# A mixture-of-experts stage: first blocks at fixed places, padding from two hardware DMA queues, late weights and the Gelu table asked for early

## The reference, cut to what matters

```python
deg = max((adj != 0).sum(-1), 1)
x = x + relu((a_norm(adj, deg) @ ln(x) + ln(x)) @ W + b)          # graph layer
xf = ln(x)
logits = xf @ Wr + br                                             # 16 experts
topk_w, topk_idx = top_k(softmax(logits), 2); topk_w /= topk_w.sum()
for e in range(16):
    h = gelu(xf @ W1[e] + b1[e])          # 256 -> 512
    o = h @ W2[e] + b2[e]                 # 512 -> 256
    y = y + combine[:, e:e+1] * o
x = x + xf + y
```

## Time and profile before

| | |
|---|---|
| median of three runs | 675.21 us |
| the profiled execution: its time / its span | 674.82 us / 673.2 us |
| TensorE busy | 601.6 us (89%) |
| VectorE, GpSimd, ScalarE busy | 456.5, 351.9, 232.0 us |
| graph layer ends, about | 338 us |
| first block's transposes, T(0) | 362.97 us |
| mean granted TensorE clock | 0.970 |

### The profile page before, as it was taken

One profiled execution on the slowest core, in us unless ns is written; L12 is line 12 of the kernel. 1 busy time (PEld: TensorE's weight loads), 2 busy tenths in 40 slices (PEclk: granted clock), 3 DMA queues, 4 the chain that ended last, 5 costly groups with the idle time before them and its releaser, 6 DMA issues. The chain is left out here.

```text
span 673.2 us, 17554 instructions
## 1 busy us (share of the span) xinstructions
PE 601.6 (89%) x4798; PEld 464.8 (69%) x4799; DVE 456.5 (68%) x1372; ACT 232.0 (34%) x482; POOL 351.9 (52%) x390
## 2 busy tenths in 40 slices
PE   2999999999999999999924899998999999999993
PEld 1777888888888788888811566665667767677772
DVE  2755788888888888889871567675765566566561
ACT  2785333333323332323320343433333323332331
POOL 6232566666777566665457245444345344344443
PEclk9999999999999999999965899999999999999997
DMA  9908799999999999997274357656734443443410
GB/s 237 225 10 157 141 198 196 197 194 192 189 193 191 194 175 186 190 192 177 90 294 131 81 130 155 139 116 141 143 66 82 76 76 65 69 73 65 80 34 2
DMA packets 65918, 93.25 MB, mean 139 GB/s; under 512 B 9547, under 2 KB 40559, under 8 KB 65360
## 3 DMA queue, kind: packets, MB, share of 16 engines
q0 software_dynamic: 33696, 51.87, 46.0%
q1 hardware_dynamic: 31600, 39.76, 19.0%
q10 hardware_dynamic: 576, 1.05, 0.5%
HBM read 103.71 MB, written 25.83 MB: 192 GB/s over the span
## 5 line engine op out<-in xcount | busy, mean ns | idle before, releaser
L459 PE MATMUL bank<-wall,at_xg 128*128 128x257 f16 x1024 | 238.6, 274 | 5.9 <-DVE at_xg L801 5.8
L461 PE MATMUL bank<-wall,at_xg 128*128 128x256 f16 x1024 | 233.1, 273 | 0.0
L1272 POOL DMA_INDIRECT out_dram<-orows,at_xg x79 | 128.5, 1626 | 165.6 <-DMA out_dram<-orows,at_xg 112.5
L563 PE MATMUL bank<-wall,feat 128*128 x474 | 118.6, 387 | 10.9 <-issue 9.0
L459 PEld LDWEIGHTS bank<-wall,at_xg 128*128 128x128 f16 x1024 | 102.8, 100 | 27.9 <-DVE at_xg L801 13.8
L1100 DVE SCALAR_TENSOR_TENSOR hl<-bank,xseT 128x512 f16<-128x512 f32 x79 | 54.6, 691 | 92.2 <-ACT xseT L744 92.2
L1238 POOL DMA_INDIRECT rows<-feat,posi x64 | 66.8, 1044 | 91.1 <-issue 90.8
L738 ACT ACTIVATE hgs<-hgs 128x512 f32<-128x512 f32 x79 | 49.8, 630 | 185.4 <-DVE hgs L1094 185.4
L461 PEld LDWEIGHTS bank<-wall,at_xg 128*128 128x128 f16 x1024 | 100.3, 98 | 15.0
L586 PE MATMUL bank<-wall,xseT 128*128 x632 | 109.1, 274 | 0.0
L563 PEld LDWEIGHTS bank<-wall,feat 128*128 128x128 f16 x474 | 46.5, 98 | 59.1 <-issue 25.5
(11 more groups left out here) (149 smaller groups left out, 826.5 us busy)
## 6 DMA issues: line engine op xcount, KB each, us to landing
abuf<-in_adj_dram POOLq DMA_DIRECT2D x128, 256.0 KB, 6.6
wst<-in_L_ffn_W_dram SPq DMA_DIRECT2D x32, 512.0 KB, 4.7
at_xg<-rows SPq DMA_DIRECT2D x79, 136.0 KB, 2.4
out_dram<-orows SPq DMA_DIRECT2D x32, 128.0 KB
abuf<-in_L_ffn_b_dram SPq DMA_DIRECT2D x4, 1024.0 KB, 10.2
wall<-in_x_dram SPq DMA_DIRECT2D x12, 256.0 KB, 13.2
out_dram<-orows,at_xg POOLq DMA_INDIRECT x79
wall<-in_x_dram ACTq DMA_DIRECT2D x4, 256.0 KB, 6.3
```

The source lines that it names most:

```text
L459: both = [lambda: pe.matmul(ps_acc[odd][:, 0:D + 1], w, yh[:, j, 0:D + 1], start=j == 0, stop=j == T - 1), lambda: pe.matmul(ps_acc[odd][: ...
L461: lambda: pe.matmul(ps_acc[odd][:, 0:D], w, yl[:, j, :], start=False, stop=False)]
L563: mm = pe.matmul(q_h[r % 2][:, :], a, w, start=n == 0, stop=n == 3 * DC - 1)
L1272: L.indirect_dma_start(out, bass.IndirectOffsetOnAxis(ap=info[r][:, 0:1].bitcast(U32), axis=0), orow[r], None, bounds_check=N - 1, oob_is_ ...
```

## The change: what it does

Every expert's region grows by 128 rows (`ROOM = CAP + P`), so that a padding write of 128 rows always fits. The first eight blocks are the first blocks of experts 0 to 7, always, at row r x ROOM; an expert without tokens gets a block of pad rows. Their row and expert are constants in the program. The table covers only the 71 blocks after them. The padding is one plain DMA of 128 rows per expert, whose row is read from a register: experts 0 to 3 by SP, 4 to 7 and 8 to 15 by ScalarE. SP asks for the first two late weight transfers right behind its last store of the graph layer. ScalarE runs one tiny Gelu before its padding writes. The adds of the first eight blocks each wait for the add before.

```diff
-FIRST = 2
+PADS = ((0, 4), (4, 8), (8, 16))
+ROOM = CAP + P
+    def fixed(q):
+        return isinstance(q, int) and q == 0
+    def write_pads(eng, which):
+        eng.wait_ge(ev("counted_out"), 1)
+        for e in range(*PADS[which]):
+            at_place = eng.value_load(pad_at[0:1, e:e + 1], min_val=e * ROOM, max_val=e * ROOM + CAP)
+            eng.dma_start(rows[bass.ds(at_place, P), :], pad[:, :]).then_inc(padded[which], 16)
+    def after_pads(eng, which):
+        first, end = PADS[which]
+        eng.wait_ge(padded[which], 16 * (end - first))
# SP
-        sp.wait_ge(ev("table_made"), 1)
-        after(sp, "pads_table", 0)
-        for odd in (0, 1):
-            sp.wait_ge(listed[odd], 16 * TOPK * T // 2)
-        sp.wait_ge(ev("multiplied"), T * CH)
-        sp.wait_ge(ev("padded_first"), 16 * FIRST)
         def load_block(q, r):
             if not isinstance(q, int) or q > 0:
                 after_added(sp, q - 1, r)
+            if fixed(q):
+                row = r * ROOM
+            else:
                 passed(sp)
-            row = sp.value_load(tab[0:1, bass.ds(blk(q, r), 1)], ...)
-            pads = sp.value_load(pads_before[0:1, bass.ds(blk(q, r), 1)], ...)
-            sp.wait_ge(ev("padded"), pads)
-            passed(sp)
+                row = sp.value_load(tab[0:1, bass.ds(in_table(q, r), 1)], ...)
...
+            if is_block(nxt, 0, PADS[1][0]):
+                after_pads(sp, 1)
+            if is_block(nxt, 1, 0):
+                after(sp, "table_made", 0)
+                sp.wait_ge(ev("spare_pads"), 16)
+                after_pads(sp, 2)
...
         load_late(0)
         load_late(1)
+        write_pads(sp, 0)
+        for odd in (0, 1):
+            sp.wait_ge(listed[odd], 16 * TOPK * T // 2)
+        sp.wait_ge(ev("multiplied"), T * CH)
+        after_pads(sp, 0)
# TensorE, ahead of T(0)
-        pe.wait_ge(ev("table_made"), 1)
+        after(pe, "table_made", 0)
+        after(pe, "earlier_made", 0)
# ScalarE, behind the last tile
+        act.activation(warm[:, :], mhalf[:, 0:1], ACT.Gelu).then_inc(ev("gelu_warm"), 1)
+        write_pads(act, 1)
+        write_pads(act, 2)
# VectorE
+        V.tensor_copy(pad_at[:, :], ps_P[0:1, 0:E]).then_inc(ev("counted_out"), 1)
-        V.scalar_tensor_tensor(out=padi[:, :], in0=padf[:, 0, :], scalar=float(PLACES), in1=padf[:, 1, :], ...)
...
+        V.tensor_scalar(nblk[:, :], nblk[:, :], 0.0, None, ALU.max).then_inc(ev("table_step"), 1)
# GpSimd
-        for e in range(E):
-            L.indirect_dma_start(rows, ...padi[:, e:e + 1]..., pad[:, :], ...)
...
         def add_results(q, r):
             after(L, "weighted", blk(q, r))
             if not isinstance(q, int) or blk(q, r) >= 2:
                 after_added(L, *shift(q, r, -2))
-            if not isinstance(q, int) or blk(q, r) >= 1:
+            if fixed(q):
+                if r >= 1:
+                    L.wait_ge(added[(r + 1) % 2], 16 * ((r + 1) // 2))
+            else:
                 others = L.value_load(earlier[...], ...)
                 L.wait_ge(added[(r + 1) % 2], others)
```

More of the change, by code:

```diff
@@ L74 @@
 LATE = 4
-PLACES = E * CAP + P
+ROOM = CAP + P
+PLACES = E * ROOM + P
 RW = 272
@@ L161, in build @@
     rowinfo = feat[:, :, :, D:D + 2]
-    padf = sb("padf", [P, 2, E], F32)
-    padi = sb("padi", [P, E], I32)
+    pad_at = sb("pad_at", [1, E], I32)
+    warm = sb("warm", [P, 1], F32)
     base = [orows[:, 7 - k, :] for k in range(2)]
@@ L232, in build @@
     listed = [sem(f"listed{c}") for c in range(2)]
+    padded = [sem(f"padded{k}") for k in range(len(PADS))]
     xg_in = [sem(f"xg_in{c}") for c in range(U)]
@@ L318, in blk, with is_block, in_table @@
         return q * U + r
+    def fixed(q):
+        return isinstance(q, int) and q == 0
+    def is_block(at, q, r):
+        return isinstance(at[0], int) and at == (q, r)
+    def in_table(q, r):
+        return blk(q, r) - U
+    def write_pads(eng, which):
[6 more added lines that the diff above has]
+        eng.wait_ge(padded[which], 16 * (end - first))
     block = ctx.enter_context(nc.Block())
@@ L588, in expert_out @@
             mm.then_inc(ev("expert_out"), 1)
-        pe.wait_ge(ev("table_step"), 12)
-        after(pe, "pads_known", 0)
-        for k, c in enumerate((3, 4, 6)):
+        pe.wait_ge(ev("table_step"), 14)
+        for k, c in enumerate((3, 4)):
             mm = pe.matmul(ps_R[0:1, k * P:(k + 1) * P], tbl[:, c:c + 1], id32[:, :], start=True, stop=True)
@@ L1017, in _ @@
         V.wait_ge(ev("table_step"), 2)
-        V.tensor_scalar(padf[:, 0, :], cnt[:, :], 2.0 ** 23, float(P), ALU.subtract, ALU.mult).then_inc(ev("pad_step"), 1)
-        V.tensor_scalar(padf[:, 1, :], run[:, :], iota_p[:, 0:1], None, ALU.add).then_inc(ev("pad_step"), 1)
-        V.wait_ge(ev("pad_step"), 2)
-        V.tensor_tensor(padf[:, 0, :], padf[:, 1, :], padf[:, 0, :], ALU.is_ge).then_inc(ev("pad_step"), 1)
-        V.wait_ge(ev("pad_step"), 3)
-        V.scalar_tensor_tensor(out=padi[:, :], in0=padf[:, 0, :], scalar=float(PLACES), in1=padf[:, 1, :],
-                               op0=ALU.mult, op1=ALU.add).then_inc(ev("pads_placed"), 1)
         V.scalar_tensor_tensor(out=nblk[:, :], in0=cnt[:, :], scalar=2.0 ** 23, in1=first_block[:, :],
@@ L1067, in _ @@
         after(V, "earlier_step", 2)
-        V.tensor_scalar(tbl[:, 5:6], tbl[:, 5:6], 16.0, None, ALU.max).then_inc(ev("earlier_ready"), 1)
+        V.tensor_scalar(tbl[:, 5:6], tbl[:, 5:6], 16.0 * U / 2, None, ALU.add).then_inc(ev("earlier_ready"), 1)
         after(V, "earlier_T", 0)
@@ L1087, in expert_of @@
         def expert_of(q, r):
-            return V.value_load(tab[0:1, bass.ds(blk(q, r) + P, 1)], min_val=0, max_val=E - 1)
+            if fixed(q):
+                return r
+            return V.value_load(tab[0:1, bass.ds(in_table(q, r) + P, 1)], min_val=0, max_val=E - 1)
         def bias1(q, r, e):
@@ L1172, in _ @@
         L.tensor_copy(firsts[:, :], run[:, :]).then_inc(ev("constants"), 1)
-        L.iota(first_block[:, :], [[CAP // P, E]], base=0, channel_multiplier=0, allow_small_or_imprecise_dtypes=True)\
-         .then_inc(ev("constants"), 1)
+        for half in (0, 1):
+            L.iota(first_block[:, half * EARLY:E - EARLY + half * EARLY], [[ROOM // P, EARLY]],
+                   base=half * EARLY * ROOM // P + 1 - half, channel_multiplier=0,
+                   allow_small_or_imprecise_dtypes=True).then_inc(ev("constants"), 1)
         L.memset(mhalf[:, :], -0.5).then_inc(ev("constants"), 1)
@@ L1203, in _ @@
         after(L, "pad_made", 0)
-        L.dma_start(rows[E * CAP:PLACES, :], pad[:, :]).then_inc(ev("padded"), 16)
+        L.dma_start(rows[E * ROOM:PLACES, :], pad[:, :]).then_inc(ev("spare_pads"), 16)
         L.wait_ge(ev("constants"), CONSTANTS)
@@ L1251, in _ @@
         over_tiles(L, step)
-        after(L, "pads_placed", 0)
-        L.wait_ge(ev("padded"), 16)
-        passed(L)
-        for e in range(E):
-            L.indirect_dma_start(rows, bass.IndirectOffsetOnAxis(ap=padi[:, e:e + 1].bitcast(U32), axis=0), pad[:, :], None,
-                                 bounds_check=PLACES - 1, oob_is_err=False).then_inc(ev("padded_first" if e < FIRST else "padded"), 16)
         for k in range(2):
@@ L1267, in add_results @@
                 after_added(L, *shift(q, r, -2))
-            if not isinstance(q, int) or blk(q, r) >= 1:
-                others = L.value_load(earlier[0:1, bass.ds(blk(q, r), 1)], min_val=16, max_val=16 * BLOCKS)
+            if fixed(q):
+                if r >= 1:
+                    L.wait_ge(added[(r + 1) % 2], 16 * ((r + 1) // 2))
+            else:
+                others = L.value_load(earlier[0:1, bass.ds(in_table(q, r), 1)], min_val=16 * U // 2, max_val=16 * BLOCKS)
                 L.wait_ge(added[(r + 1) % 2], others)
@@ L1274, in add_results @@
              .then_inc(added[r % 2], 16)
-        after(L, "earlier_made", 0)
         def bstep(q, r):
             prev2 = shift(q, r, -2)
+            if is_block(prev2, 1, 0):
+                after(L, "earlier_made", 0)
             if exists(*prev2):
```

35 lines of the change are left out of this document (17 added, 18 removed).

## The result

| | before | after |
|---|---|---|
| median, on one chip | 675.08 us (674.72 to 676.76) | 668.57 us (667.01 to 669.86) |
| ratio, 95% interval | | 0.9897 [0.9878, 0.9916] |
| the profiled execution: its time / its span | 674.82 / 673.2 us | 667.72 / 666.1 us |
| mean granted clock | 0.970 | 0.977 |

The change takes 6.5 us off; 3.0 us were forecast. Run again on two other chips it gave 668.42 us against 672.23 (0.9942 [0.993, 0.9955]) and 668.79 against 672.52 (0.9944 [0.9923, 0.9965]). The changed kernel's medians agree within 0.4 us, those of the kernel before do not: 675.1 us here, 674.6 and 674.8 us in two measurements on one other chip, 672.1 to 672.5 us on three more. So the gain is 3.7 to 6.5 us.

What follows compares the result with a forecast made beforehand. The hand-over to the experts was taken as bound by GpSimd's padding, then DMA latency and a slow clock, TensorE only after 380 us. 674.82 - 5.2 - 4.1 + 8.1 - 1.8 = 671.8 us, median 672.2; range 664.5 to 680.5 us.

Steps and rivals of the forecast that it cites:

- term 1: Start of the experts: block 0's transposes, T(0), come at 357.8 us instead of 362.97, 5.2 us off.
- term 3: Adds 0 to 9: serial adds L = 5.4 us apart make block 17's transposes, T(17), later, 8.1 us on.
- term 2: Block 3's transposes, T(3): the 2.65 us wait for padding and a half-clock stretch go, 4.1 us off.
- term 4: Later serial adds, blocks 15 and 16 before: half of the 3.6 us lost from T(22) to T(26) goes, 1.8 us off.
- Dear serial adds: Adds 0 to 9: serial adds take more than the start gives, L = 6.2, 680 us; chance 0.22.
- Free adds: Adds 0 to 9: the adds cost nothing, term 3 is zero from L = 4.6 down, 664 us; chance 0.12.
- ScalarE's writes: ScalarE's padding writes at 1.5 us each make the first Gelu 3.2 us late, 676 us; chance 0.15.
- The clock falls in the chain: T(12) to T(17): TensorE's waits halve its clock, 1.4 us more in each of five steps, 679 us; chance 0.08.

Runs made afterwards that it cites:

- latew: Changed kernel with the first two late weight transfers back ahead of the first block load, behind the padding: 672.11 us, 0.9952 of 674.77.
- earlyw: Kernel before with only the first two late weight transfers asked for right behind SP's last store: 673.16 us, 1.002 of 672.23.
- before_again: Kernel before, unchanged, run once more for a second profile: 674.81 us, 1.0001.
- noweights: Changed kernel without the late weight transfers except expert 8's two, so experts 9 to 15 use stale weights: 664.54 us, 0.9855.
- fulladd: Changed kernel with the adds of blocks 1, 3, 5 and 6 going to 128 different rows, as if full: 672.49 us, 0.9966 of 674.6.
- after_again: Changed kernel, unchanged, run once more on another chip: 668.42 us, 0.9942 of 672.23.
- tableread: Changed kernel without fixed blocks, padding writes dealt out otherwise on SP and ScalarE, register reads ahead of waits for adds: 665.07 and 665.59 us, 0.9851 and 0.9895.
- readfirst: Changed kernel with register reads of block loads and adds put ahead of the waits for earlier adds: 667.39 us, 0.9933.
- splitread: Changed kernel with SP and ScalarE sharing the first four padding writes, SP doing the last eight after its first loads, and register reads first: 666.92 us, 0.9918.
- tablesplit: Changed kernel with all 79 blocks from the table, SP and ScalarE sharing the first four padding writes, SP doing the last eight later: 668.46 us, 0.9945.
- even_after: Changed kernel without the router's bias, so every expert has 421 to 668 tokens: 672.56 us, 0.9975.
- split: Changed kernel with SP and ScalarE sharing the first four padding writes, SP doing the last eight behind its first loads: 668.2 us, 0.9947 of 672.07.

## Why the prediction was off in size

The direction was right, and so was the main mechanism, an earlier start against a slower chain of serial adds; the cause given for term 1 was not. The step that failed is the size of term 3: it put 8.1 us on, and 2.8 us were measured at T(17), 3.6 at T(18), since L was taken as 5.4 us and was 4.5 to 4.9. By the prediction's own steps, shifts against the first profile of the kernel before:

| | forecast | profiled |
|---|---|---|
| T(0) (term 1) | -5.2 | -2.5 |
| T(3) (with term 2) | -9.3 | -7.1 |
| T(17) (with term 3) | -1.2 | -4.4 |
| T(26) (with term 4) | -3.0 | -7.2 |
| time of the execution | -3.0 | -7.1 |

**Term 1, forecast 5.2 us, measured 2.5.** The counts came 0.5 us later than in the kernel before (VectorE's copy at 349.55 us). SP's first read took 1.0 us instead of 0.71, and the four writes were done after 4.78 us instead of 3.6 (3 x 1.08 and an issue of 0.36), so the last was issued at 355.2 instead of 353.3 us, and it landed 2.9 us later instead of 2.1. The loads went out at 358.20 us and not at 355.4. The last leg, 2.3 us to T(0), was as forecast. The row for a landing was of one write by itself; sixteen go out here within some 13 us. The reason was wrong in the main too: of the 5.2 us, 4.3 were put down to loads that go out earlier once the padding has moved, and 0.8 to the weights; latew and earlyw show that the weights alone give what there is.

**Term 2, forecast 4.1, measured 4.6.** Right: the wait at T(3) went, and the clock rose one hidden product earlier and stayed up in the changed kernel's three profiles.

**Term 3 is the step that failed.** Its formula has two parts. From add 0 to add 9 it put 48.6 us, measured 40.9, and 43.8 and 43.7 in two more profiles. From add 9 to T(17) it put 8.0 us, measured 8.9, 7.6 and 7.6. So the size of L was wrong, 5.4 against 4.5 to 4.9 (the first of these profiles is the one beside the forecast: T(17) 1.4 us further from add 0 than before, and add 0 itself only 5.7 us earlier where T(3) is 7.1). L was taken from five periods of one profile, and they do not repeat: in before_again the same five have a mean of 4.36 us instead of 5.73. Two of them, 6.18 and 6.84 us, hold a GpSimd instruction of 2.61 and 2.19 us instead of 1.56, which is 1.05 and 0.6 of the 2.1 and 2.5 us that they are longer than in before_again; how weight transfers and adds fall beside each other is what is left to explain the rest, and is not shown row by row. noweights shows what an undisturbed one takes: 4.5 to 4.75 us full, 4.0 to 4.1 with 12 or 14 tokens, 3.65 empty. By 4.75, 4.0 and 3.65 us and the known counts the nine would come to 39 us (five full or nearly, two small, two empty), and the changed kernel's three profiles have 2 to 5 us more. The reason given for going below 5.7, that four of the ten have few tokens, was right, but all reasons together took 0.3 us off each period, 3 us in all, from a base a microsecond too high. By that list the few tokens alone are worth 3.7 us; in fulladd the nine take 4.1 us more than in the first profile of the changed kernel, and 1.2 us more than in after_again.

**Term 4, forecast 1.8, measured 3.2 to 3.7** (T(22) to T(26) 15.19 us instead of 18.37; T(18) to T(26) 29.73 instead of 33.40). Nearly all of the 3.6 us went, and not half. Two serial adds in a row are not the whole reason: in before_again and in tableread they stand at the same blocks, are 3.9 to 5.4 us long, and T(22) to T(26) lose nothing. The term is what dear serial adds cost in one profile.

**The rivals.** *Dear serial adds* is dead: the changed kernel has L = 4.54, 4.87 and 4.85 in three profiles, and 5.0 only with those adds filled. *Free adds* (L from 4.6 down, 664 us) was half right: L was 4.54 in the first profile, but T(17) still waited 2.17 us. Add 9 has add 10 right behind it and a weight transfer beside (which of them matters is not shown). SP issued block 17's load at 423.79 us, 6.8 us after add 9's start, where L + 0.7 us of reading would have been 5.2. Only noweights is this case, at 664.5 us. *ScalarE's writes* is dead: twelve writes from 350.66 to 363.46 us, where 364.5 was estimated, and the first Gelu at 366.10 waits only for the bias. *The clock falls in the chain* did not come in the changed kernel: after 2.17 us of waiting T(17) takes 0.40 us, which is full clock, and the other two profiles stay at full as well. But it is a real cost of waits like these. In six profiles of variants with the same kind of waits, the granted clock went to 0.50 for some 3 us: fulladd (T(16), a wait of 2.87 us), readfirst (T(16), 2.48), splitread (T(16), 2.98), tablesplit (T(24), 2.75), latew (T(17), 1.66) and even_after (T(13), 1.97, and T(16), 2.34). The rows of readfirst and of latew, where the hidden product behind the wait takes 2.10 us instead of 1.46:

```profile
422.86 0.56 PE L568 MATMUL bank<-id,at_xg 128*128 128x128 f16 x4 [2.48 <-DMA at_xg<-rows]
```

```profile
434.41 2.10 PE L590 MATMUL bank<-wall,feat 128*128 x6
```

The wait's length alone doesn't decide it: after 2.35 us (split) and 2.17 us (the changed kernel) the clock stayed at full. From that block's transposes to the next block's it took 4.75 to 5.40 us, against 4.2 to 4.3 at full clock, so by an estimate from these a fall costs 0.5 to 1.1 us, once, where the prediction had 1.4 us in each of five steps. The Trainium skill (TensorE: Matmul & The Clock Gate, section HAM oscillation) describes a kernel in which TensorE waits some 3 to 5 us for data in every round and is throttled every time; here shorter waits do it too, but not each time.

**What stays open.** Why the kernel before takes 2.5 us less on some chips while the changed one doesn't: it wasn't profiled there. What VectorE stood still for in before_again, and what makes block 4's add dear. With the two measured legs, 40.9 and 8.9 us, in place of its own, the forecast's sum would have been a gain of 9.7 us, more than the 7.1 profiled: the dear L hid that term 1 was 2.7 us too rich. That term 3 was not zero hung on the profile it was read from: with the 4.36 us of before_again it would have been. So that the forecast missed by 4 us and not by more is luck. That weight transfers lengthen serial adds is shown by noweights; how they do, and why they did not in before_again, is not.

## What to carry to other kernels

Before you price a chain of dependent transfers by a mean of its periods, sort the periods: by how many rows each really writes, and by what stands beside it. Then look at a second profile of the same kernel: here the mean moved by 1.4 us. A large transfer that a queue was given just ahead of a small urgent one is the small one's latency; ask for it earlier, or elsewhere. And an earlier start is worth only what the next wait lets through: move both, or the second gives the first back.

## What the runs showed of the hardware

- Indirect DMAs that accumulate 128 rows of 1 KB into DRAM, each waiting for the one before, start 4.5 to 4.75 us apart, 4.0 to 4.1 us if 12 to 14 of the rows are real, and 3.65 us if none is (both noweights profiles, block 4's add apart); 5 to 7.3 us occur with the weight transfers.
- A 136 KB load lands in 2.3 us, and behind two 512 KB transfers of the same queue 6.4 to 6.7 us after these were issued.
- GpSimd's instruction for such a DMA takes 1.56 us, and 1.7 to 2.6 us where VectorE's 128x1024 `scalar_tensor_tensor` on two SBUF inputs starts within a microsecond ahead of it: it is then over 2.64 to 2.67 us after that one's start (116 adds in 20 profiles; a single one that began in the same hundredth of a microsecond took 1.56 us). The Trainium skill (VectorE: DVE Perf Modes, section Two Vector instructions with no wait between them) says in passing that the second input of such an instruction is read through an interface that VectorE shares with GpSimd; the rows agree, and no run here tries it by itself.
- Register read and DMA issue together: 1.13 us each on ScalarE's queue (eleven gaps in 12.4 us), 1.5 us on SP's (three gaps in 4.4 us).
- After waits for block rows of 1.66 to 2.98 us TensorE's granted clock fell from 1.00 to 0.50 for about 3 us in six profiles, and stayed at 1.00 after 2.17 and 2.35 us in two others.
